# Second mixture of experts: landing waits on GpSimd and another order of its gathers and scatters

## The reference, cut to what matters

```
x = tokens.reshape(2048, 256); cap = int(1.25 * 2048 / 8)        # 320 rows for an expert
top2_w, top2_idx = top_k(softmax(x @ gate_w.T), 2)               # two experts a token
keep = counts <= cap                                             # an expert with more picks than cap is dropped
buf[a_e, p] = x[tok_id]                                          # gather: rows of an expert side by side
h = silu(buf @ w1.T + b1); y = h @ w2.T + b2                     # per expert, 320 x 256
out = sum over the two picks of y[a_e, p] * weight               # scatter back, mix
x = layernorm(x + out)
```

## Time and profile before

| | us |
|---|---|
| median of 3 runs | 1129.98 |
| lowest and highest of them | 1127.99, 1132.28 |
| the profiled execution's own time | 1137.67 |
| its span, from the first to the last instruction | 1135.9 |

### The profile page before, as it was taken

One profiled execution on the slowest core, in us unless ns is written; L12 is line 12 of the kernel. 1 busy time (PEld: TensorE's weight loads), 2 busy tenths in 40 slices (PEclk: granted clock), 3 DMA queues, 4 the chain that ended last, 5 costly groups with the idle time before them and its releaser, 6 DMA issues.

```text
span 1135.9 us, 20834 instructions
## 1 busy us (share of the span) xinstructions
PE 1007.0 (89%) x8628; PEld 717.5 (63%) x8628; DVE 617.5 (54%) x1398; ACT 425.0 (37%) x557; POOL 255.6 (22%) x282
## 2 busy tenths in 40 slices
PE   6989989989988899999998798989879987986887
PEld 3666566666675798996445474656656574753656
DVE  2653753652767573333335836656574669655333
ACT  1523533524524356555431434152415423340212
POOL 0310310220120333333331120231103112103642
PEclk9999999999987899999999899999999999997999
DMA  6013412211400891111112000200110010005527
GB/s 188 1 43 112 147 43 97 98 43 65 131 1 1 326 323 44 50 48 48 38 48 84 1 6 1 85 2 5 41 34 2 6 38 1 2 1 154 153 89 235
DMA packets 64237, 80.50 MB, mean 71 GB/s; under 512 B 12736, under 2 KB 57680, under 8 KB 63120
## 3 DMA queue, kind: packets, MB, share of 16 engines
q1 hardware_dynamic: 53392, 61.15, 16.3%
q0 software_dynamic: 5664, 15.47, 4.2%
q10 hardware_dynamic: 5088, 2.56, 0.9%
HBM read 46.13 MB, written 33.03 MB: 70 GB/s over the span
## 4 chain that ended last, share of the span: by engine, by line
PE 46%; issue 21%; DVE 16%; ACT 12%; DMA 2%; POOL 2%; SPq 1%; another core or an unknown queue 1%; ACTq 0%; DVEq 0%; POOLq 0%
PE ps L1517 8%; DVE sb_arena L871 6%; ACT sb_arena L642 6%; PE ps L1653 5%; PE ps L1675 4%; PE ps L1778 3%; PE ps L1723 3%; DVE sb_arena L875 3%; PE ps L1561 2%; PE ps L1990 2%; PE ps L1625 2%; DVE ps L892 2%; PE ps L1852 1%; PE ps L1696 1%; PE ps L2005 1%
## 5 line engine op out<-in xcount | busy, mean ns | idle before, releaser
L642 ACT ACTIVATE sb_arena<-ps 77x2048 f32<-77x2048 f32 (+1 forms) x64 | 116.5, 1883 | 27.8 <-PE ps L1607 26.6
L1383 POOL TENSOR_TENSOR sb_arena<-sb_arena,sb_neghalf 128x2 f32<-128x2 f32 x40 | 28.7, 719 | 398.4 <-DVE sb_arena L837 398.4
L1517 PE MATMUL ps<-sb_arena,sb_wreg 128*128 128x256 f32 (+1 forms) x512 | 108.5, 360 | 6.8 <-issue 3.8
L1517 PEld LDWEIGHTS ps<-sb_arena,sb_wreg 128*128 128x128 f32 (+1 forms) x512 | 87.6, 192 | 23.2 <-issue 8.3
L1852 PE MATMUL ps<-sb_arena 128*128 128x128 f32 x800 | 99.3, 278 | 3.3 <-DVE sb_arena L1246 2.3
L1625 PE MATMUL ps<-sb_arena 32*77 32x256 f32 (+1 forms) x1024 | 77.6, 420 | 27.0 <-ACT sb_arena L642 14.5
L1852 PEld LDWEIGHTS ps<-sb_arena 128*128 128x128 f32 x800 | 96.0, 194 | 5.4 <-issue 3.1
L754 ACT ACTIVATE sb_arena<-sb_arena 128x1024 f32 x72 | 76.0, 1057 | 16.9 <-issue 12.3
L1625 PEld LDWEIGHTS ps<-sb_arena 32*77 32x77 f32 (+1 forms) x1024 | 43.7, 175 | 47.5 <-ACT sb_arena L642 25.6
L871 DVE TENSOR_REDUCE sb_arena<-ps 128x8 f32<-128x2048 f32 x32 | 71.0, 2282 | 3.5 <-PE ps L1581 3.5
L1561 PE MATMUL ps<-sb_headrow,sb_identb 128*32 128x512 bf16 (+1 forms) x266 | 64.7, 380 | 1.4 <-DVE sb_arena L875 1.3
(11 more groups left out here) (285 smaller groups left out, 1891.1 us busy)
## 6 DMA issues: line engine op xcount, KB each, us to landing
sb_arena<-in_m_w SPq DMA_DIRECT2D x8, 1536.0 KB, 9.5
sent<-sb_xres SPq DMA_DIRECT2D x32, 256.0 KB
sb_arena<-outs SPq DMA_DIRECT2D x16, 512.0 KB, 5.8
outs<-sb_zeros SPq DMA_DIRECT2D x4, 1664.0 KB, 9.7
sent<-sb_zeros SPq DMA_DIRECT2D x2, 2560.0 KB, 13.7
sb_arena<-in_m_w SPq DMA_DIRECT2D x16, 256.0 KB
early<-sb_xres SPq DMA_DIRECT2D x12, 256.0 KB, 2.9
sb_arena<-in_xT SPq DMA_DIRECT2D x8, 256.0 KB, 3.5
```

What stands on the lines that cost most here:

```text
L642: nc.scalar.activation(dst, src, ACT.Exp).then_inc(S(f"h_PT{p}"), 1)
L1517: ins = mm(dst[:, m * cols:(m + 1) * cols], wt[0:rows, k, m * P:(m + 1) * P], src[0:rows, k, 0:cols], start=(k == 0), stop=(k == KC - 1))
```

## The change

The loop over the experts on GpSimd is written out. The scatter of one expert becomes a function, and two waits are added: `gathered(e)` waits until the gathers of expert e (and of those before it on the same semaphore) have landed, `scattered(e)` until the scatters up to expert e have. The new order, with G for the gathers of an expert and S for its scatters, is: G0 to G3, S0, G4, G5, wait for G5, S1, G6, wait for G6, G7, S2, S3, wait for S3, S4 to S7. The waits for G0, G1, G2 and G3 stand ahead of gathers that reuse their semaphore. The number of transfers, their tiles and what PE, DVE, ACT and SP do stay the same.

```diff
--- before.py
+++ after.py
@@ -1480,15 +1480,36 @@
 
             pool.wait_ge(S("indexed"), 3)
             pool.wait_ge(S("sent1"), 16 * 2 * B)
-            for e in range(XBUFS):
-                gather1(e)
-            for e in range(E):
+            def scatter1(e):
                 for i, j in enumerate(tiles_of(e, False)):
                     pool.wait_ge(S("e_ys"), e + 1 + (i if e + 1 == E else 0))
                     g.indirect_dma_start(outs1[:, :], bass.IndirectOffsetOnAxis(ap=idx1[:, j:j + 1], axis=0), y1t[:, j, :], None
                                          ).then_inc(S("e_out"), 16)
-                if e + XBUFS < E:
-                    gather1(e + XBUFS)
+
+            def gathered(e):
+                pool.wait_ge(S(f"t_in{e % XBUFS}"), rows_at(e))
+
+            def scattered(e):
+                pool.wait_ge(S("e_out"), 16 * sum(len(tiles_of(x, False)) for x in range(e + 1)))
+
+            for e in range(XBUFS):
+                gather1(e)
+            scatter1(0)
+            for e in (4, 5):
+                gathered(e - XBUFS)
+                gather1(e)
+            gathered(5)
+            scatter1(1)
+            gathered(2)
+            gather1(6)
+            gathered(6)
+            gathered(3)
+            gather1(7)
+            scatter1(2)
+            scatter1(3)
+            scattered(3)
+            for e in range(4, E):
+                scatter1(e)
             for b in range(B):
                 ln = lnrow[:, b]
                 pool.wait_ge(S("vars"), b + 1)
```

## The result

The changed kernel takes 1134.32 us (median of 20 executions, 1128.92 to 1140.13), the kernel before 1131.49 (20, 1127.24 to 1136.54): a ratio of 1.0031, interval 1.0015 to 1.0046. By the ratio that is about 3.5 us slower, by the medians 2.8; it is inside half a percent, where I forecast 1130.0 and no change. The time lies 0.8 us above my range, and 4.3 above my forecast: 1.5 of that is the kernel before itself (1131.49 in these executions, 1129.98 in the three that I had), 2.8 is the change.

A forecast was written before the change was run, and what follows sets the result against it. PE, 89% busy, bounds the kernel. Its 6.96 us of lateness was taken as recording only and the 4.4 us of waits as hidden before S7, leaving the unrecorded 1129.98 at 1130.0, range 1122 to 1133.5.

The forecast's parts named there:

- The steps of PE: Second mixture: starts of experts' second matmuls become 5.97 and 5.78 us apart throughout, removing 6.96 us of long steps.
- Recorded against unrecorded executions: Whole kernel: 1137.67 recorded against 1129.98 unrecorded, 7.69 us, of which 6.96 would be lateness existing only while recording.
- A: PE's late signals belong to the recorded execution; timed runs already undisturbed, waits hide before S7: 1130 us, chance 0.56.
- B: PE's lateness is real in every run, starts near a run's eighth transfer, runs of 7 remove it: 1123.0, chance 0.25.
- The three landing waits: GpSimd, waits for G5, G6 and S3: 1.46 us each, 4.4 together, bounds 0 to 9.4.
- The cover ahead of S7: GpSimd ready for S7 at 1097.9, DVE's outputs allow it at 1099.34: 1.4 us left, so the waits hide.
- rival D: GpSimd becomes the bound of the last scatters through slower landings: 1131 to 1136 us, chance 0.10.
- my own bounds: GpSimd's three biting waits: from 0 to three times the longest idle stretch of a wait, 3.13, so 9.4 us.
- Moved gathers and scatters: GpSimd's new order: gathers still in time, only the last scatter waited for; worth nothing.
- The profiled execution: Recorded profile of the changed kernel: own time near 1131 us, PE's mixing starting near 1108.6.

The follow-up runs named there:

- e1: Kernel before, unedited, timed and profiled once more: ratio 1.001 to its other executions, 1130.6 us at equal clock.
- e8: Kernel before, unedited, profiled a third time: ratio .9995, 1130.7 us at equal clock.
- e10: Kernel before, unedited, in a set whose traces lack landings of indirect transfers: ratio .9995, 1135.0 us at equal clock.
- e15: Changed kernel, unedited, again in a set whose traces lack landings: ratio .9988 to the kernel before, 1133.7 us at equal clock.
- e11: Changed kernel, unedited, in a set whose traces lack landings: ratio .998 to the kernel before, 1133.7 us at equal clock.
- e9: Changed kernel with weight loads of experts 4 to 7 cut to 16 of 128 rows: ratio .9971 to the kernel before, 1130.8 us at equal clock.
- e16: Changed kernel with gathers first in each run, so the three waits follow scatters; traces lack landings: ratio .9975 to the kernel before, 1131.7 us at equal clock.
- e17: Kernel of e16 repeated, again in a set whose traces lack landings: ratio .9937 to the kernel before, 1131.5 us at equal clock.
- e2: Changed kernel, unedited, timed and profiled again: ratio 1.0018 to the kernel before, 1133.0 us at equal clock.
- e5: Changed kernel without its last wait, for S3: ratio .9998 to the kernel before, 1130.3 us at equal clock.
- e6: Changed kernel with three more waits, after S4, S5 and S6: ratio 1.0069 to the kernel before, 1137.7 us at equal clock.
- e18: Kernel of e16 a third time, in a set whose traces have landings: ratio 1.0016 to the kernel before, 1131.9 us at equal clock.
- e3: Changed kernel without its three biting waits, new order only: ratio 1.001 to the kernel before, 1131.2 us at equal clock.
- e4: Kernel before in its old order, with landing waits after G4, S2 and S3: ratio .9998, 1132.1 us at equal clock.
- e7: Changed kernel reordered to issue all 20 gathers, then the scatters, 30 transfers without a pause: ratio 1.0004 to the kernel before, 1130.4 us at equal clock.
- e12: Kernel of e5, unedited, in a set whose traces lack landings: ratio 1.003 to the kernel before, 1136.1 us at equal clock.
- e13: Kernel of e3, unedited, in a set whose traces lack landings: ratio 1.0065 to the kernel before, 1139.9 us at equal clock.
- e14: Kernel of e7, unedited, in a set whose traces lack landings: ratio 1.0086 to the kernel before, 1142.6 us at equal clock.

## Why the prediction was wrong, step by step

**The steps of PE**: right for the profile of the changed kernel. 5.97 and 5.78 throughout, no "remote" wait, no low clock among the experts. In the timed set there was most likely nothing to remove: before has no long step in either of its profiles from condition 1 (e1, e8).

**Recorded against unrecorded executions** (where I chose A): wrong. None of the timed executions is known to be unrecorded. What separated 1137.67 from 1129.98 was mostly the condition in which they ran (1135.9 against 1130.3 to 1130.7 at equal clock), and for the rest the clock. My A said "the timed runs have undisturbed steps", and for the timed set of the result that held, for a reason other than mine: e1 and e8 show it with profiles of before. My B ("real, starts with the eighth or so transfer, cut by runs of 7") is what e10 to e15 show in condition 2. Its price there was not 6.96 net: at equal clock the changed kernel gains 1.6 (e11 and e15), since it pays the waits. The rule of the Trainium skill (page "NOTIFIC — the notification-queue block", section "Overflow: three behaviours, one of which stalls the engine") would make the lateness a work of the recording. The traces of condition 2 lack records (6,651 to 6,800 semaphore records a trace, against 7,982 to 7,997 in condition 1); whether that has to do with the lateness no run shows. All executions of a kernel with long runs are slow in those sets, and every one of them carries a span and a clock, so none is known to be without recording; the rule is neither shown nor excluded.

**The three landing waits**: the failed step of the time. I took 2.45 us for a gather's landing and 1.46 for the wait. Both landings that I measured had no weight load beside them. With the loads of SP beside them the first two waits add 3.3 and 2.9. The third adds 1.9, beside no load but beside two packets of the instruction queues; without those it adds 1.4 in e9, e16 and e17. Together that is 8.1 instead of 4.4. e9 cuts the loads to an eighth, and the sum falls to 4.9; of the fall, 0.6 lies in the third wait and is not the loads' doing.

**The cover ahead of S7**: the working was right, its input wrong. Without waits the slack (the time that GpSimd can lose before S7 is late) is 5.8 us (27 transfers, 34.7, against 40.6 from S0 to S7), and S7 is late by what the waits add beyond it:

| run | waits add | less 5.8 | S7 late, measured |
|---|---|---|---|
| changed | 8.1 | 2.3 | 2.06 |
| e2 | 8.0 | 2.1 | 1.90 |
| e5 | 6.2 | 0.4 | 0.17 |
| e6 | 13.2 | 7.4 | 7.18 |
| e9 | 4.9 | none | 0.00 |
| e11 | 7.9 | 2.1 | 1.90 |
| e15 | 7.9 | 2.1 | 2.03 |
| e16 | 6.1 | 0.3 | 0.00 |
| e17 | 6.7 | 0.9 | 0.56 |
| e18 | 8.3 | 2.5 | 2.21 |

In e9, e16 and e17 PE itself is 0.30, 0.87 and 0.17 late into expert 6, which widens the slack by as much.

So rival D was the mechanism in condition 1: 1.2 us longer a landing (3.7 over three) gives "GpSimd becomes the bound of the last scatters". I gave it 0.10, and said myself that it decides from 0.5 us more a landing. It should have weighed more: the longest idle stretch of a wait in my own bounds, 3.13 a wait, was nearer to the truth than the value I took.

**Moved gathers and scatters**: worth nothing alone within the error (e3), as said; but see e4 for what they do for the waits.

**The profiled execution**: forecast near 1131, PE's mixing at 1108.6; found 1136.08 and 1113.80. Of these 5.2 us, 2.6 come from a first gather at 1045.77 instead of 1043.18, ahead of anything that the change touches, 1.8 lie from the last expert to the mixing (S7's 2.06, less a shorter load), and 0.8 between the first gather and the first L2011 (12.03 us against 11.20). That last stretch does not follow the kernel: it took 11.15 to 12.03 us over all profiles, 11.15 in before (e1) and 12.02 in the changed kernel (e2), but 12.03 in e4 and 11.20 in the changed kernel again (e15).

**What stays open.** In condition 1 the changed kernel is 2.7 to 3.0 us slower and S7's lateness accounts for 2.0 of it; the rest, 0.7 to 0.9, is the size of the error. e3, with the new order and S7 on time, has 0.8 over before too, but e5, with the same order, has none. A stretch of low clock at the start of the mixture was 13.7 us in e1, e3, e5, e6 and 17.1 in e2, e4, e7, e8 (before and after: 13.7 and 17.1): it does not follow the change. Why a packet of an instruction queue falls into the third pause in some kernels and not in others stays open too. What condition 2 is, and whether the lateness in it belongs to the chip or to its recording, no kernel here could show.

## What to carry to other kernels

Before a profile is read for a stall, compare its own time with the timed runs at the same granted clock, and see whether its transfers have landings: a profile can come from another condition than the times. A wait for a landing costs what the landing takes beside whatever shares the DMA engines at that moment, so measure the landing there and not in a quiet stretch. Then add up all waits on an engine against its slack at the one place where somebody waits for it; what exceeds the slack arrives at the end almost one for one. Last, look at what a pause holds before giving it a cause: the third wait was short of loads and still long.

## What the runs showed of the hardware

- A gather of 128 rows of 1 KB landed in a median of 2.8 us, a scatter in 2.4; beside weight loads GpSimd idled 3.65 and 3.19 us for the last one of a run of gathers, and 1.98 and 2.23 with those loads cut to an eighth. In e18 it idled 3.25 and 3.35 for the last scatter of a run beside such loads.
- From the issue of the last scatter of a run to the next issue, with no load beside it, took 2.66 to 2.69 us in six pauses, and 2.97 to 3.56 in the six that also held one packet of each of two instruction queues.
- In one condition, long runs of indirect transfers issued without a pause beside PE's work made DVE and ACT start late behind PE: runs of ten and more with experts still to come gave long steps of 3.6 to 14.6 us in sum (two profiles of the kernel before, one each of e12, e13 and e14), runs of seven 0 to 0.9; DVE's waits without a releaser were 4.1 us in e12 and 12.3 in e14. In the other condition, 30 did nothing. The ten gathers up to the first expert's L1990 did nothing in either.
- Behind 3.23 us without PE work twelve matmuls took 4.57 us in before that otherwise take 3.0, in a stretch at the lower clock; behind 12.90 us idle in e14 they took 4.63.
